# A macaron block (two expert FFNs around a selective scan) on one core: products, sums and statistics moved between the two halves of a chunk

## What is computed

```
x = x + 0.5 * ffn(layernorm(x))          # "f1"
x = x + attn(layernorm(x))               # "p"
x = x + 0.5 * ffn(layernorm(x))          # "f2"

ffn(x):   expert = argmax(x @ Wg + bg)   # 8 experts
          h = gelu(x @ W1[e] + b1[e]); y = h @ W2[e] + b2[e]; take y of the token's expert
attn(x):  xn = rmsnorm(x); x_path, z = split(xn @ in_proj.T)
          x_path = silu(conv4(x_path)); dt_x, B, C = split(x_path @ x_proj.T)
          dt = softplus(dt_x @ dt_proj.T + b)
          h = exp(dt*A) * h + dt * x_path * B;  y = sum_n(h * C) + D * x_path   # 256 steps, 16 states
          return (y * silu(z)) @ out_proj.T + x
```

## Time and profile before

| | us |
|---|---|
| median of 3 runs | 1582.62 (1580.9 to 1586.93) |
| the profiled execution, its own time | 1583.12 |
| its span, first to last instruction | 1581.2 |
| PE busy (weight loads 594.1 beside it) | 1197.0, 76% of the span |
| POOL busy | 1067.5, 68% |
| DVE busy | 1063.0, 67% |
| ACT busy | 876.8, 55% |
| mean granted TensorE clock | 0.862 of full speed |

### The profile page before, as it was taken

One profiled execution on the slowest core, in us unless ns is written; L12 is line 12 of the kernel. 1 busy time (PEld: TensorE's weight loads), 2 busy tenths in 40 slices (PEclk: granted clock), 3 DMA queues, 4 the chain that ended last, 5 costly groups with the idle time before them and its releaser, 6 DMA issues.

```text
span 1581.2 us, 16257 instructions
## 1 busy us (share of the span) xinstructions
PE 1197.0 (76%) x5188; PEld 594.1 (38%) x5188; DVE 1063.0 (67%) x1713; ACT 876.8 (55%) x1171; POOL 1067.5 (68%) x900
## 2 busy tenths in 40 slices
PE   3777757597787868787777869877786868768677
PEld 1333414243433434343433434433443434324344
DVE  2022788867767687877777677777777686979920
ACT  0234646555665757465665746465665757474522
POOL 1026697958667777867777777877768777888610
PEclk9968778788897989989898989889898999788677
DMA  3005050503222220413222220413222230514000
GB/s 79 1 0 195 9 187 9 186 9 110 83 102 100 85 104 23 165 35 109 87 102 100 98 91 22 149 47 114 87 102 93 74 115 16 179 57 145 1 7 14
DMA packets 60405, 130.02 MB, mean 82 GB/s; under 512 B 7744, under 2 KB 26864, under 8 KB 52128
## 3 DMA queue, kind: packets, MB, share of 16 engines
q1 hardware_dynamic: 60320, 128.98, 23.8%
HBM read 106.94 MB, written 22.02 MB: 82 GB/s over the span
## 4 chain that ended last, share of the span: by engine, by line
PE 43%; DVE 23%; ACT 22%; issue 7%; POOL 4%; SPq 1%; ACTq 0%; DVEq 0%; DMA 0%; POOLq 0%
PE PH L447 11%; DVE dA L727 10%; PE PY L463 10%; PE G L435 8%; ACT hs L586 7%; PE Y L477 5%; DVE hb L731 4%; PE PH L446 3%; ACT dA L605 3%; ACT L587 3%; ACT hs L578 2%; DVE xs L744 2%; DVE hb L725 2%; ACT L586 2%; PE G L499 1%
## 5 line engine op out<-in xcount | busy, mean ns | idle before, releaser
L904 POOL TENSOR_TENSOR hb<-dtx_rep,bs 128x1024 f32<-128x1024 f32 x256 | 598.1, 2356 | 0.4 <-PE Y L477 0.4
L727 DVE TENSOR_TENSOR_SCAN dA<-dA,hb 128x512 f32<-128x512 f32 x352 | 429.3, 1220 | 60.6 <-ACT dA L605 56.4
L605 ACT ACTIVATE dA<-dt_rep,A 128x512 f32<-128x512 f32 x512 | 342.0, 690 | 205.8 <-DVE hb L731 195.4
L578 ACT COPY hs<-PH 128x512 f32<-128x512 f32 x256 | 149.7, 585 | 388.1 <-PE PH L447 387.7
L463 PEld LDWEIGHTS PY<-W,hs 128*128 128x128 f32 x2048 | 286.5, 207 | 172.3 <-issue 161.2
L463 PE MATMUL PY<-W,hs 128*128 128x128 f32 x2048 | 338.0, 306 | 0.0
L447 PE MATMUL PH<-xnT,W 128*128 128x512 f32 x512 | 333.0, 736 | 0.0
L912 POOL TENSOR_TENSOR hb<-hb,cs 128x1024 f32<-128x1024 f32 x80 | 188.5, 2356 | 175.9 <-DVE hb L725 175.9
L725 DVE TENSOR_TENSOR_SCAN hb<-dA,hb 128x512 f32<-128x512 f32 x160 | 186.8, 1209 | 135.2 <-ACT dA L605 132.5
L731 DVE TENSOR_TENSOR hb<-dA,cs 128x512 f32<-128x512 f32 x352 | 243.5, 692 | 25.2 <-DVE dA L727 0.9
L446 PE MATMUL PH<-ohT,Lm 24*128 24x512 bf16 x256 | 108.9, 425 | 158.0 <-ACT hs L578 157.5
(11 more groups left out here) (85 smaller groups left out, 1180.7 us busy)
## 6 DMA issues: line engine op xcount, KB each, us to landing
dtx_rep<-dtx_rows SPq DMA_DIRECT2D x32, 1024.0 KB, 6.7
dt_rep<-dt_rows SPq DMA_DIRECT2D x32, 1024.0 KB, 8.2
bs<-bc_rows SPq DMA_DIRECT2D x64, 256.0 KB, 3.6
cs<-bc_rows SPq DMA_DIRECT2D x64, 256.0 KB, 4.5
dtx_rows<-dtx SPq DMA_DIRECT2D x32, 256.0 KB, 2.5
dt_rows<-dt SPq DMA_DIRECT2D x32, 256.0 KB, 2.6
X<-in_x SPq DMA_DIRECT2D x16, 256.0 KB, 3.1
out<-X SPq DMA_DIRECT2D x16, 256.0 KB, 2.4
```

What stands on the lines that cost most here:

```text
L578: nc.scalar.copy(hs[:, w, e, :], PH[:, :]).then_inc(ph_free, 1)
L605: nc.scalar.activation(dA[u % NA][:, :], dt_rep[:, h, g, :], ACT.Exp, scale=A[:, h, g, q:q + 1]).then_inc(decay, 1)
L727: nc.vector.tensor_tensor_scan(a, a, x_in_hb, 0.0, ALU.mult, ALU.add).then_inc(scan, 1)
L904: nc.gpsimd.tensor_tensor(hb[:, s % HR], dtx_rep[:, h, 2 * m:2 * m + 2, :], bs[:, q, None, :].broadcast_to([P, 2, CH]), ALU.mult).then_inc ...
```

## The change

Six edits, all in the order of work; the arithmetic is the same, but for the order in which `Y` is added up.

- The D product leaves `sum_states` and gets slots of its own, 8 and 12 (`D_AT`), in the middle of the accumulation. The sum of slots 0 and 1 (and of 8 and 9) now starts the bank.
- Second products of f1 go to slots 4, 6, 8 (three), 9 (three), those of f2 to 10, 11, 12, 13, 14 (two), 15 (two).
- First products skip slots 0 and 8: f2 has slots 1, 2, 3 (two), 4, 5, 6, 7 and f1 9, 10, 11, 12 (two), 13, 14, 15. A second one in a slot comes at the slot's end.
- `POOL_C` changes from (1, 3, 5, 9, 14) to (3, 9, 11, 12, 14).
- f1's statistics move on DVE from 12.0 to 2.5 of the same iteration, and x is loaded one iteration earlier for them; the addition of f2 moves from 2.0 to 1.5.
- `taps` waits for one more sum (6 for 5).

```
-DVE_AT = {"gated1": 1.5, "y_f2": 2.0, "gate_f1": 3.0, ...
-          "y_f1": 10.0, "stats_p": 10.5, "gate_f2": 11.0, "stats_f1": 12.0, ...
+DVE_AT = {"gated1": 1.5, "y_f2": 1.5, "gate_f1": 3.0, ...
+          "y_f1": 10.0, "stats_p": 10.5, "gate_f2": 11.0, "stats_f1": 2.5, ...
-W1_AT = [[(8 + e, 3) for e in range(E)], [(e, -2) for e in range(E)]]
-W2_AT = [[(2 + e, 2) for e in range(E)], [(10 + e, -2) if e < 6 else (e - 6, -3) for e in range(E)]]
+W1_AT = [[(s, k, 3) for s, k in ((9, 0), (10, 0), (11, 0), (12, 0), (12, 1), (13, 0), (14, 0), (15, 0))],
+         [(s, k, -2) for s, k in ((1, 0), (2, 0), (3, 0), (3, 1), (4, 0), (5, 0), (6, 0), (7, 0))]]
+W2_AT = [[(s, 2) for s in (4, 6, 8, 8, 8, 9, 9, 9)], [(s, -2) for s in (10, 11, 12, 13, 14, 14, 15, 15)]]
+D_AT = {8: 0, 12: 1}
-POOL_C = (1, 3, 5, 9, 14)
+POOL_C = (3, 9, 11, 12, 14)
...
-                it.wait(sp_, x_out, 4 - XR, 16, 16)
-                it.wait(sp_, x_in, 4, 16, 0)
+                it.wait(sp_, x_out, 5 - XR, 16, 16)
+                it.wait(sp_, x_in, 5, 16, 0)
...
-                    nc.tensor.matmul(Y[:, :], Dd[:, h, :], xs[:, (it.i0 + off) % 2, h]..., start=True, stop=False)
...
-                                            start=False, stop=q == NQ - 1)
+                                            start=q == 0, stop=q == NQ - 1)
...
+                    if s in D_AT and it.has(0):
+                        nc.tensor.matmul(Y[:, :], Dd[:, D_AT[s], :], xs[:, it.i0 % 2, D_AT[s]]...,
+                                         start=False, stop=False)
+                    for unit in w2_units(s):
+                        second_product(it, *unit)
+                    for unit in w1_units(s, 1):
+                        first_product(it, *unit)
...
-                    it.wait(act, summed, 0, 8, 5)
+                    it.wait(act, summed, 0, 8, 6)
...
+                it.wait(dve, moments[w], off, 1, 0)
```

More of the change, by code:

```diff
@@ L57 @@
           "ln_f2": 9.5, "ln_p": 13.5, "taps": 14.5, "gelu_f1": 15.5}
-DVE_AT = {"gated1": 1.5, "y_f2": 2.0, "gate_f1": 3.0, "out": 5.5, "oh_f1": 6.0, "stats_f2": 6.0, "gated0": 9.5,
-          "y_f1": 10.0, "stats_p": 10.5, "gate_f2": 11.0, "stats_f1": 12.0, "oh_f2": 13.0, "tap01": 15.0, "tap2": 15.5}
+DVE_AT = {"gated1": 1.5, "y_f2": 1.5, "gate_f1": 3.0, "out": 5.5, "oh_f1": 6.0, "stats_f2": 6.0, "gated0": 9.5,
+          "y_f1": 10.0, "stats_p": 10.5, "gate_f2": 11.0, "stats_f1": 2.5, "oh_f2": 13.0, "tap01": 15.0, "tap2": 15.5}
 POOL_AT = {"root_f2": 6.5, "norm_f2": 7.0, "dt": 8.0, "dtx": 8.5, "root_p": 11.0, "norm_p": 12.0, "root_f1": 12.5,
@@ L63, with w1_units, w2_units @@
          "c2": 14, "dt1": 15, "c3": 15}
-W1_AT = [[(8 + e, 3) for e in range(E)], [(e, -2) for e in range(E)]]
-W2_AT = [[(2 + e, 2) for e in range(E)], [(10 + e, -2) if e < 6 else (e - 6, -3) for e in range(E)]]
+W1_AT = [[(s, k, 3) for s, k in ((9, 0), (10, 0), (11, 0), (12, 0), (12, 1), (13, 0), (14, 0), (15, 0))],
+         [(s, k, -2) for s, k in ((1, 0), (2, 0), (3, 0), (3, 1), (4, 0), (5, 0), (6, 0), (7, 0))]]
+W2_AT = [[(s, 2) for s in (4, 6, 8, 8, 8, 9, 9, 9)], [(s, -2) for s in (10, 11, 12, 13, 14, 14, 15, 15)]]
+W1_ORDER = sorted((s, k, w, e, off) for w in range(2) for e, (s, k, off) in enumerate(W1_AT[w]))
+W1_PLACE = {(w, e): n for n, (_, _, w, e, _) in enumerate(W1_ORDER)}
+D_AT = {8: 0, 12: 1}
 LN_OFF = {0: 3, 1: -1}
-POOL_C = (1, 3, 5, 9, 14)
+POOL_C = (3, 9, 11, 12, 14)
 NP = len(POOL_C)
 NV = UN - 2 * NP
[L76 to L83, removed]
+def w1_units(s, place):
+    return [(w, e, off) for at, k, w, e, off in W1_ORDER if (at, k) == (s, place)]
+def w2_units(s):
+    return [(w, e, off) for w in range(2) for e, (at, off) in enumerate(W2_AT[w]) if at == s]
 def g_uses(i, name):
@@ L93, in g_uses, with w1_uses @@
         n += b == bank and 0 <= i + off < NCH
-def w1_uses(i, s):
-    offs = [w1_unit(k)[2] for k in range(SLOTS)]
+def w1_uses(i, w, e):
+    offs = [off for *_, off in W1_ORDER]
     n = sum(0 <= k + off < NCH for k in range(FIRST, i) for off in offs)
-    return n + sum(0 <= i + off < NCH for off in offs[:s])
+    return n + sum(0 <= i + off < NCH for off in offs[:W1_PLACE[w, e]])
 def on_pool(s):
@@ L145, in wait_free, with wait_unit @@
             eng.wait_ge(g_free[G_AT[name][0]], n)
-    def wait_units(self, eng, sem, s, k):
-        n = w1_uses(self.i0, s) + k
+    def wait_unit(self, eng, sem, w, e, k):
+        n = w1_uses(self.i0, w, e) + k
         if n > 0:
@@ L390, in body @@
                         store_x(it)
-                    if s == SP_AT["x_in"] and it.has(4) and it.i0 + 4 > 0:
+                    if s == SP_AT["x_in"] and it.has(5) and it.i0 + 5 > 0:
                         load_x(it)
@@ L436, in product, with first_product @@
                 last.then_inc(g_full[b], 1)
-            def first_product(it, s):
-                w, e, off = w1_unit(s)
+            def first_product(it, w, e, off):
                 if not it.has(off):
@@ L442, in first_product, with second_product @@
                 if e == 0:
-                    it_oh = it if w == 0 else it.before()
-                    it_oh.wait_read(pe, g_free, f"oh_f{w + 1}")
-                it.wait_units(pe, ph_free, s, 0)
+                    made = it if w == 0 else it.before()
+                    made.wait_read(pe, g_free, f"oh_f{w + 1}")
+                it.wait_unit(pe, ph_free, w, e, 0)
                 nc.tensor.matmul(PH[:, :], Lm[:, e, :], ohT[:, w, :], start=True, stop=False)
                 nc.tensor.matmul(PH[:, :], W1[:, e, :], xnT[:, w, :], start=False, stop=True).then_inc(ph_full, 1)
-            def second_product(it, s):
-                w, e, off = w2_unit(s)
+            def second_product(it, w, e, off):
                 if not it.has(off):
@@ L471, in sum_states @@
                     it.wait(pe, gated, off, HF, h)
-                    nc.tensor.matmul(Y[:, :], Dd[:, h, :], xs[:, (it.i0 + off) % 2, h].rearrange("p b l -> p (b l)"),
-                                     start=True, stop=False)
                 it.wait(pe, prod, off, NV, on_dve(4 * k + 4))
@@ L545, in body @@
                     stages(it, s, 0)
-                    first_product(it, s)
+                    for unit in w1_units(s, 0):
+                        first_product(it, *unit)
                     stages(it, s, 1)
@@ L551, in body @@
                         sum_states(it, 0, (s - 3) // 2)
-                    second_product(it, s)
+                    if s in D_AT and it.has(0):
+                        nc.tensor.matmul(Y[:, :], Dd[:, D_AT[s], :],
+                                         xs[:, it.i0 % 2, D_AT[s]].rearrange("p b l -> p (b l)"),
+                                         start=False, stop=False)
+                    for unit in w2_units(s):
+                        second_product(it, *unit)
+                    for unit in w1_units(s, 1):
+                        first_product(it, *unit)
                     stages(it, s, 2)
@@ L569, in copy_out, with take_first @@
                 nc.scalar.copy(dst, G[b][0:rows, :]).then_inc(g_free[b], 1)
-            def take_first(it, s):
-                w, e, off = w1_unit(s)
+            def take_first(it, w, e, off):
                 if not it.has(off):
@@ L576, in take_first @@
                 it.wait(act, w2_done[w], off - 1, E, e + 1)
-                it.wait_units(act, ph_full, s, 1)
+                it.wait_unit(act, ph_full, w, e, 1)
                 nc.scalar.copy(hs[:, w, e, :], PH[:, :]).then_inc(ph_free, 1)
             def gelus(it, w):
-                off = W1_AT[w][0][1]
-                it.wait_units(act, ph_free, W1_AT[w][-1][0], 1)
+                it.wait_unit(act, ph_free, w, E - 1, 1)
                 for k in range(2):
@@ L660, in body @@
                     stages(it, s)
-                    take_first(it, s)
+                    for unit in w1_units(s, 0):
+                        take_first(it, *unit)
                     off, t = (s + LEAD_X) // SLOTS, (s + LEAD_X) % SLOTS
```

2 lines of the change are left out of this document (1 added, 1 removed).

## The result

The changed kernel takes **1624.05 us** (median of 4 runs, 1622.3 to 1624.61), the kernel before 1582.34 us beside it. The ratio is 1.0257, with a 95% interval of 1.0234 to 1.0279: 2.6% **slower**, 13 us above the upper end of the range. The profiled execution took 1623.76 us, its span is 1621.9 us against 1581.2, and the mean granted clock is 0.823 against 0.862.

A forecast was written before the change was run, and what follows sets the result against it. No one engine was full before; POOL would take the place of PE and DVE. Thirteen steady iterations at 0 to +0.3 us give +2, the run-in -2: 1583.1 + 2 - 2 = 1583 us, range 1560 to 1611.

The forecast's parts named there:

- slower rival: PE falls to half clock in its new waits, mainly the 4 us for POOL: 1603 us, chance 0.29 (0.30 with spread).
- (b): First half: slot 1 leaves POOL_C, DVE multiplies by C itself, about 1.5 us; sum 0.9 us late at the gating.
- (f): Slot 5 leaves POOL_C: 1.5 us more ahead of "out", "bc" and the first half 0.7 us later; bounds nothing and 1.5.
- (a): Slot 0: ACT no longer copies a first product, a copy of 0.59 us; slot 1 starts 0.6 us earlier.
- (e): First half: ACT's silu begins at 781.42 behind a decay, so it stays, and so does slot 5 at 787.43.
- (d): f1's statistics come behind slot 2, some 1.25 us of DVE's; sum level, -0.1 to +0.1 us at slot 3.
- (c): First half: PE's last sum is ready early; DVE's waits of 1.64 and 0.48 us go, 1.2 us early behind the addition.
- (h): Slot 8: DVE's waits of 1.63 and 0.85 us go; DVE and POOL's root 2.3 us early, the gain an iteration.
- (i): Second half: DVE saves 1.5 us in slot 11, 1.5 in slot 12 and 1.25 of statistics: 6.5 us early at slot 13.
- (j): Second half: PE's sum waits for POOL's slot 11 product until 834.9; last x product starts at 839.3, against 838.89.
- The run-in: Filling the pipe: DVE gets f1's last second product some 1 us earlier in each of two iterations, -2 us.
- The faster one: Rival: slow stretches at half clock leave the path, 1571 us, or 1558 with POOL earlier; chance 0.28 (0.31 with spread).

## Why the prediction was wrong, point by point

The forecast was no change, and the slower rival 1603 us; both were too low. The steps that failed are (b) and (f), DVE's products by C of slots 1 and 5: (f) was entered with +0.7 us for the whole first half, and the 1.5 us of (b) as cancelled ahead of the silu. Measured, the half got 2.5 us longer in eight of the eleven steady iterations, slot 5 on DVE costs 48 us and slot 1 17.

- **(a) to (e) held as a sum, and hid two costs.** Slot 3 starts 17.7 us behind slot 0 in both kernels, the silu load 20.2 us. But (e) read the silu as a fixed point, "so it stays, and so does slot 5". With slot 1 on POOL again, in the old `POOL_C` or with slots 11 and 12 beside it, it comes at 18.6 to 19.7 us in most iterations; with slot 5 alone back it stays at 20.2. So it moves with DVE. (b) and (d) had cancelled (a) and (c), and the balance looked like an anchor. That is why 17 us for slot 1 and 15 for the statistics were counted as nothing. I compared the whole change with before, and not each edit with the change without it, as a sum over several edits should.
- **(f) had the time and not the clock.** "bc" is 0.9 us late, for 0.7 forecast (1.5 us more, less the 0.6 us in hand, is 0.9 by the prediction's own figures). But the rest of the half was to "follow as before", and it followed at 0.50: the gelu of f2 is loaded at 45.1 for 42.6, 2.5 us late. This is the mis-sized term: +0.7 us, measured +2.5, 1.6 of it the clock, in iterations 3 to 6 and 8 to 11.
- **The point from which the clock falls was put wrong.** The slower rival "decides from a wait between 2.6 and 5.2 us on", from two rows. Behind 2.36 us ahead of "bc" it fell in eight steady iterations, and behind 2.25, 2.31 and 2.36 us it did not in iterations 2, 7 and 12. Two rows had shown two cases, and I read a threshold in the length of the wait between them; these rows have both outcomes at one length. What decides instead no run here shows.
- **(h) was right on the waits and wrong on what they leave.** DVE waits for neither sum nor `PY`; both are done while ACT is in its gelu. POOL's root starts 60.8 us behind slot 0 for 61.5 before, 0.7 us early for the 2.3 forecast; the difference is about the 1.8 us that the first half lost beyond (f). Counted from the gelu the root is 3.2 us earlier (15.7 for 18.9), where the forecast has 3.0: the gain is there. But with this work gone ahead, PE stands still 3.35 us for the copy of the layernorm, a gap that the list of new waits didn't have, and then is at half clock for 13.7 us. In before PE had a first product, the sum and a second product to do there behind the gelu, at half clock for 5.5 us, and was at full speed from some 816 us on:

```profile
810.74 0.60 PE L446 MATMUL PH<-ohT,Lm 24*128 24x512 bf16 x1 [5.28 <-ACT hs L578]
...
816.63 0.96 PE L519 MATMUL G<-Wg,xnT 128*128 128x8 f32 x8
```

  Moving work forward into a wait of another engine opened a gap behind it.
- **(i) did not come about.** DVE was to be 6.5 us early at slot 13, and is there 72.1 us behind slot 0, for 72.0 before. It saves the work, and waits 2.01, 2.16 and 1.40 us for decays behind ACT's copies of slow first products.
- **(j) is a true floor, and rarely reached.** POOL's product ends at 75.2 us behind slot 0 and the sum starts at 76.05, in order with no wait, since PE was later still. Where PE is at full speed or iterations are short the wait appears: in iterations 0 and 1, in the fill of slot 10, and in the old kernel with the new `POOL_C`, there with 4.51 us. The sum had this wait right, but priced thirteen iterations by one of them. Iterations 0, 1, 13 and 14 lost 21 us, half of the result. In the first two and in 13 the wait shows, and it accounts for 13 us, which the run with slots 11 and 12 on DVE has back; the other 8 us are not from it.
- **The run-in** gained 6.5 us for the 2 of the sum, **the run-out** lost 6.3 for nothing forecast.
- **The rivals.** The slower one has the right mechanism, PE at half clock in its new waits, but placed it behind the wait for POOL only and named a "thinner first half" without a price. The faster one asked whether the slow stretches leave the path; in after the one behind the gelu of f2 grew from 6.8 to 13.7 us. With the old `POOL_C` it would have been right in its sign, at 1549.

Settled by the runs: the new `POOL_C` loses more than the whole result, slot 5 above all, and half of slot 5's part is the clock. Not settled: what part of slot 1's 17 us and of the statistics' 15 is clock and what is DVE's time, as no run filled the gaps with these alone; and why the run-in gained as much as it did.

## What to carry to other kernels

Cost each edit of a change against the change without it, also where the sum is nothing: two shifts that cancel in front of a wait look like a fixed point, and hide that one of the edits gains what the other loses. Where work leaves an engine's gap, list the gap that opens behind it, not only the waits that close, and price the matmuls behind it at both levels of the clock. A few matmuls without use in a suspected gap are a cheap test: if the kernel gets faster with more work, the clock was on the path; if not, look for the wait that came in its place.

## What the runs showed of the hardware

- TensorE stayed at half clock (0.51, its 1.2 GHz level) through a stretch of 14 us in which it was busy all the time, with tiles from 128 x 8 to 128 x 512, and at 0.50 for 13.7 us in the run with the old `POOL_C`; a full row of busy time doesn't say that the clock is up. The Trainium skill, TensorE: Matmul & The Clock Gate, "The HAM clock gate (the "warmup" mystery)", has the throttled clock as the default that activity releases; three of the fills, which add 128 x 512 matmuls and nothing else, agree with it: -41, -40 and -26 us. The 14 us show that being busy was not enough here to release it.
- At the end of the kernel, first products of 1.4 us with waits of 0.73 us between them fell to half clock in both kernels: in the changed one behind two such waits, in the one before behind four, in the last two products.
- What a fill does differs with its place and with what waits there: -26 us in slot 6, nothing in slot 10 with the new `POOL_C`, -40 in slot 10 with the old one, nothing around slot 1.
- The same wait ahead of the same product was followed by either speed: 2.36 us and then "bc" in 2.67 us in iteration 5, 2.36 us and then 1.88 us in iteration 12.
- POOL's products by C took 2350 ns at the median in after (2335 to 2370), 2356 in before, with 32 of the 80 at new places. The 66 that overlap a scan of DVE have a median of 2349 ns, the other 14 of 2352: no contention is seen. It also could not be expected from the rule that the prediction quotes, which asks for two inputs in SBUF: in this kernel a scan and a product by C on DVE read `dA`, which is in PSUM, and so have one. The rule was read wrongly there.
